# Expert numbers loaded twelve at a time on TensorE, row numbers four at a time on SyncE

## The reference

```
weights, indices = _gate(xt, gate_w)          # 4 experts of 16 for each of the 4096 tokens
h1 = jnp.einsum('td,edi->tei', xt, w1)
h3 = jnp.einsum('td,edi->tei', xt, w3)
a = jax.nn.silu(h1) * h3
y = jnp.einsum('tei,eid,te->td', a, w2, c)
z = jax.nn.silu(xt @ ws1) * (xt @ ws3) @ ws2
```

## Time and profile before

| | |
|---|---|
| median of the runs | 646.26 us (640.41 to 646.84) |
| span of the profiled execution | 669.7 us |
| expert stage in it | 272.6 to 551 us |
| PE busy | 512.2 us, 76% of the span |
| DVE busy | 428.0 us, 64% |
| ACT busy | 303.6 us, 45% |
| POOL busy | 289.2 us, 43% |
| DMA in the expert stage | 0.57 to 0.88 of the 16 engines, turn by turn |

### The profile page before, as it was taken

The page is one execution under the profiler, slowest core; times in us unless marked ns, Lnnn a source line. Parts: engine busy times, 40 slices in busy tenths (PEclk is TensorE's granted clock), DMA queues, the critical chain, the costliest instruction groups (busy, mean ns, idle before and its releaser), DMA issues.

```text
span 669.7 us, 13463 instructions
## 1 busy us (share of the span) xinstructions
PE 512.2 (76%) x3532; PEld 356.3 (53%) x3555; DVE 428.0 (64%) x1200; ACT 303.6 (45%) x659; POOL 289.2 (43%) x334
## 2 busy tenths in 40 slices
PE   1899897697889768879898878878989799645500
PEld 1355454354554435767787666767868675311300
DVE  2446874657766487767677444567878774653784
ACT  3526554245452434456666555655756563101100
POOL 1000107273753720345455330245656464776573
PEclk9999898697998899999999999999999999877755
DMA  7022256354653220378788887578798864342232
GB/s 200 27 79 80 70 182 236 134 188 159 259 199 140 79 86 1 118 246 261 235 283 286 284 282 245 181 238 265 242 298 256 273 218 138 90 131 81 95 119 101
DMA packets 64091, 118.63 MB, mean 177 GB/s; under 512 B 9760, under 2 KB 23088, under 8 KB 64048
## 3 DMA queue, kind: packets, MB, share of 16 engines
q1 hardware_dynamic: 51216, 84.55, 38.5%
q0 software_dynamic: 12288, 33.57, 15.7%
q10 hardware_dynamic: 544, 0.00, 0.0%
HBM read 55.17 MB, written 62.91 MB: 176 GB/s over the span
## 4 chain that ended last, share of the span: by engine, by line
PE 37%; DVE 17%; issue 13%; SPq 10%; DMA 7%; another core or an unknown queue 6%; ACT 5%; POOL 4%; ACTq 0%; DVEq 0%; POOLq 0%
PE t L1346 5%; PE h_even L1155 4%; PE h_even L1157 3%; PE h_even L1156 3%; PE y L1192 3%; DMA kv<-expert_in 3%; PE h_odd L1157 3%; PE h_odd L1155 3%; SPq L327 3%; PE h_odd L1156 3%; DVE x_all L1061 2%; SPq L330 2%; SPq L334 2%; ACT x_all L516 1%
## 5 line engine op out<-in xcount | busy, mean ns | idle before, releaser
L440 POOL DMA_INDIRECT expert_in<-x_all,slots x128 | 129.5, 1012 | 119.8 <-PE h_even L1157 59.5
L459 POOL DMA_INDIRECT wa_stage<-expert_out,result_of x64 | 64.2, 1004 | 39.0 <-issue 14.0
L1346 PE MATMUL t<-ident,kv 128*128 128x128 f32 x384 | 58.5, 275 | 16.2 <-DMA kv<-expert_in 11.7
L1050 DVE TENSOR_TENSOR wa_lo<-bias_heads,wa_hi 128x256 bf16<-128x256 f32 x96 | 40.6, 423 | 46.2 <-ACT wa_hi L648 35.5
L426 POOL TENSOR_SCALAR neg_mean<-mv 128x4 f32<-128x4 f32 x16 | 4.9, 309 | 132.7 <-DVE mv L705 132.5
L459 POOL DMA_INDIRECT q_fm<-expert_out,result_of x32 | 32.2, 1007 | 57.9 <-PE h_odd L1157 34.0
L1031 DVE TENSOR_TENSOR xsT_lo<-t,xsT_hi 128x512 bf16<-128x512 f32 x72 | 49.4, 687 | 11.2 <-ACT xsT_hi L623 6.2
L1346 PEld LDWEIGHTS t<-ident,kv 128*128 128x128 f32 x384 | 43.6, 141 | 23.5 <-issue 11.9
L1155 PE MATMUL h_even<-xsT_hi,we_hi 128*128 128x256 f16 x192 | 52.3, 273 | 0.1
L1156 PE MATMUL h_even<-xsT_lo,we_hi 128*128 128x256 bf16 x192 | 52.3, 273 | 0.0
L1157 PE MATMUL h_even<-xsT_hi,we_lo 128*128 128x256 f16 x192 | 52.3, 273 | 0.0
(11 more groups left out here) (222 smaller groups left out, 1498.9 us busy)
## 6 DMA issues: line engine op xcount, KB each, us to landing
kv<-expert_in SPq DMA_DIRECT2D x96, 256.0 KB
expert_out<-k_exp SPq DMA_DIRECT2D x48, 256.0 KB
expert_out<-q_exp SPq DMA_DIRECT2D x48, 256.0 KB
expert_in<-wa_stage SPq DMA_DIRECT2D x16, 512.0 KB
expert_in<-wa_stage SPq DMA_DIRECT2D x32, 256.0 KB
stage<-in_L_ffn_w SPq DMA_DIRECT2D x48, 128.0 KB
x_in<-in_L_attn_x SPq DMA_DIRECT2D x8, 512.0 KB
out<-gated SPq DMA_DIRECT2D x8, 512.0 KB
```

Source lines behind the costliest of these rows:

```text
L440: pool.indirect_dma_start(xs_dram[b // WB], bass.IndirectOffsetOnAxis(ap=slots[:, b, t, j:j + 1], axis=0), x_all[:, b, t, :], None).then_i ...
L459: pool.indirect_dma_start(y_got[i][:, j, :], None, ys_dram[w], bass.IndirectOffsetOnAxis(ap=result_of[:, b, t, j:j + 1], axis=0)).then_inc ...
L1050: dve.tensor_tensor(aT_lo[r % 2][:, :], a_pair, aT_hi[r % 2][:, :], ALU.subtract).then_inc(at_lo_ready, 1)
L1346: last = pe.transpose(t_bank[r % 2][:, c * 2 * P + i * P:c * 2 * P + (i + 1) * P], xs[r][:, i, c * P:(c + 1) * P], ident[:, :])
```

## The change

On TensorE `chunk_of` goes and `chunks_of(first, n)` comes: one load instruction that fills n registers from n words that lie side by side. A turn calls it once, at its start, for 12 pairs: the two last of the turn before, its own eight, and two more that it does not use. Turn 0 loads 8. On SyncE `ring_rows(w, q)` loads the four row numbers of a group ahead of the group's first `load_xs`. The call checks every value that it loads, as the single load did.

```
-            def load_xs(w, p, r, first=False):
-
-                row = sp.value_load(pair_row[0:1, NPAIR * w + p, :], min_val=0, max_val=SLOTS - PAIR)
+            def ring_rows(w, q):
+
+                return nc.values_load_multi_w_load_instructions(
+                    pair_row[0:1, bass.ds(NPAIR * w + RING * q, RING), 0], engines=[mybir.EngineType.SP],
+                    min_val=0, max_val=SLOTS - PAIR)[1]
+
+            def load_xs(w, p, r, row, first=False):
+
                 if not first:
                     sp.wait_ge(xs_transposed, NPAIR * w + p - RING + 1)
...
+                rows = ring_rows(w, q + 1)
                 for r in range(RING):
-                    load_xs(w, RING * (q + 1) + r, r)
+                    load_xs(w, RING * (q + 1) + r, r, rows[r])
...
-            def chunk_of(g):
-                return pe.value_load(pair_chunk[0:1, g, :], min_val=SHARED, max_val=NCH - 1)
+            def chunks_of(first, n):
+
+                return list(nc.values_load_multi_w_load_instructions(
+                    pair_chunk[0:1, bass.ds(first, n), 0], engines=[mybir.EngineType.PE],
+                    min_val=SHARED, max_val=NCH - 1)[1])
...
-                chunks = [chunk_of(RING * q)]
+                if late(q, 1):
+                    chunks = chunks_of(RING * q - RING, 3 * RING)[RING - 2:]
+                else:
+                    chunks = [None, None] + chunks_of(0, 2 * RING)
                 for i in range(2 * RING):
...
-                    up_pair(g, r, chunks[i])
-                    if i < 2 * RING - 1:
-                        chunks.append(chunk_of(g + 1))
-                    if i >= 2:
-                        down_pair(g - 2, (r - 2) % RING, chunks[i - 2])
-                    elif late(q, 1):
-                        down_pair(g - 2, (r - 2) % RING, chunk_of(g - 2))
+                    up_pair(g, r, chunks[i + 2])
+                    if i >= 2 or late(q, 1):
+                        down_pair(g - 2, (r - 2) % RING, chunks[i])
                 return chunks[-2:]
```

More of the change, by code:

```diff
@@ L357, in _ @@
             sp.wait_ge(kv_summed, NB)
+            rows = ring_rows(0, 0)
             for r in range(RING):
-                load_xs(0, r, r, first=True)
+                load_xs(0, r, r, rows[r], first=True)
             group(0, 0, first=True)
@@ L371, in _ @@
             sp.wait_ge(zero_filled[1], FILLED)
+            rows = ring_rows(1, 0)
             for r in range(RING):
-                load_xs(1, r, r)
+                load_xs(1, r, r, rows[r])
                 store_ys(0, RING * last + r - 3, (r + 1) % RING)
+            rows = ring_rows(1, 1)
             for r in range(RING):
-                load_xs(1, RING + r, r)
+                load_xs(1, RING + r, r, rows[r])
                 if r < RING - 1:
```

## The result

The changed kernel is slower: 678.32 us, the median of 4 runs (676.81 to 680.16), beside 646.19 us for the kernel before in the same session, a ratio of 1.050 with a 95% interval of 1.046 to 1.054. The prediction was 693 us in a range of 649 to 708, with "slower" at 0.76. A ratio here is formed from a kernel's runs in the faster of its two states alone, while a median is of all its runs, so the two need not agree to the last digit.

The account below looks back on a forecast made before the run. PE was taken to bound the expert stage, lacking in good part its sequencer's register work. Longer start gaps and lost clock, less gaps removed, summed to +48.6 us on 669.7, scaled to +47, or 693 us; range 649 to 708.

Parts of the forecast that it names:

- rival (c): Turn starts: checks in a row run at 0.15 us each, start gap 2.3 us, no clock lost: 638 us; chance 0.10.
- I take word by word, 2.6 us: TensorE's load of twelve reads each word separately, so eleven more words add 2.6 us at a turn's start; chance 0.52.
- The price of a piece, 0.24 us: Register loads: the read of each word was taken as 0.24 us, from SyncE's single load of 0.27 us.
- 6.3: PE's idle gap at each turn's start in us: 0.65 + 3.1 for checks + 2.6 for the load.
- the sum: Changes over all turns of the expert stage added up: +48.6 us on the profiled 669.7 us, 7.3%.
- SyncE's 51.8: Turns 4 and 5: SyncE would need 55.4 - 3.6 = 51.8 us after its grouped loads, PE 55.2.
- No longer slower than the others: Expected sign in the profile: turns 4 and 5, 55.4 us together before, would stop being slower than the other turns.
- Rival (b): Turn starts: load of twelve costs as one, 3.7 us gap leaves the clock full: +3, 649 us; chance 0.16.
- 12 x 1.7 = 20: Clock term: behind each turn's start gap PE runs at half clock for 3.3 us, losing 1.7 us a turn.
- 0.9 us a group: SyncE: grouping a group's four loads takes 2.4 instead of 3.3 us, saving 0.9 us, 1.8 a turn.
- rival (a): Turn starts: load of twelve costs as one, gap 3.7 us, clock falls: +18.4, 664 us; chance 0.22.
- the forecast's own range: Whole kernel: 680 to 708 us, for 0.20 to 0.27 us a word and the clock low once or twice a turn.

Follow-up runs that it names:

- Experiment 4: Changed kernel with the load of twelve kept, but each check moved to where its value is next used, ten checks a turn: 638.55 us, ratio 0.982 to the kernel before.
- experiment 6: Changed kernel with the load of twelve kept and TensorE's checks of its values left out: 632.96 us, ratio 0.981 to the kernel before.
- the second profile of before: The kernel before, unedited, profiled once more: 645.21 us, span 643.5 us, against a span of 669.7 us in its first profile.
- the earlier trace: The trace of the kernel before that the prediction read, span 669.7 us; PE's clock fell behind a 4.1 us gap there.
- experiment 3: Changed kernel with TensorE's loads put back to one for each pair, SyncE's grouped loads kept: 645.63 us, ratio 0.999 to the kernel before.
- experiment 5: Changed kernel with two loads a turn, six values at its start and four ahead of its fifth pair, all checked at once: 665.06 us, ratio 1.032 to before.
- experiment 9: Changed kernel with 26 further checked loads of 1 to 12 values ahead of turn 0; only load lengths were asked for, such as 0.86 us for an aligned twelve.
- experiment 11: Changed kernel with three aligned loads of four a turn, each check where its value is next used: 669.56 us beside 666.25 for the kernel before, ratio 1.004.
- 12: Changed kernel with three aligned loads of four a turn and no checks on TensorE or SyncE: 654.9 us beside 666.25 for the kernel before, ratio 0.977.
- experiment 7: Changed kernel with a load of three values at a turn's start, then single checked loads behind each `up_pair`: 647.08 us, ratio 0.999 to the kernel before.
- experiment 8: Changed kernel with the load of twelve and its checks done twice at the start of each loop turn and the last: 733.52 us in a single run.
- experiment 10: Changed kernel with unread matmuls of 512 columns between a turn's twelve checks: 690.55 us beside 666.25 for the kernel before, ratio 1.033.

## Why the prediction came out as it did

**Where and in which form: right.** The loss is all in the expert stage, in one gap at each turn's start in front of the transposes, put down to issue. The gaps ahead of `down_pair` are gone, the waits for rows are fewer. The checks are 0.28 us apart also in a row, which leaves rival (c) without its condition. Experiment 4 shows by moving the checks, and 6 by leaving them out, that they carry the loss.

**The load of twelve: mis-sized.** The step that failed is "I take word by word, 2.6 us". The price of a piece, 0.24 us, was right; that four values can be one piece was not seen. The eleven further values cost 0.86 - 0.31 = 0.55 us. The start gap became 3.8 us on average in turns 1 to 11 instead of 6.3: 2.05 of the difference is this term. The other half microsecond is probably that a start had hardly any gap before on average (the second profile of before has 1.0 us in all, not 0.65 each as in turn 7).

**The near hit is in part luck.** With 0.55 in the sum, nine turns lose 2.05 us less each, 18.5; turn 0, whose load of eight took 0.79 us, 1.2 less; and in turns 4 and 5 PE would need 51.1, so that SyncE's 51.8 would bind: another 3.4 less. The sum is then 48.6 - 18.5 - 1.2 - 3.4 = 25.5, or 671 us on the median. So the load was some 22 us too much, and the rest of the sum some 7 us too little; the forecast is 15 off because the two have opposite signs.

**By turns**, after against the second profile of before:
- Turns 2, 3, 7, 8, 9: 125.8 against 108.3 us, +17.5 (predicted +28.3). A turn is 25.2 instead of 27.6, less by the 2.5 us of the gap.
- Turns 1, 6, 10: 79.3 against 70.6, +8.7 (predicted +10.9, or 4.8 with the right load). Turn 10 still waits 4.1 us for rows, which the sum let pass in the start gap.
- Turns 4, 5: 55.1 against 53.7, +1.5 (predicted -0.2, with 55.2 for PE). The long start is nearly free there: 8.8 us of start gaps came, while the waits for rows fell from 6.5 to 1.4 us and the gaps ahead of `down_pair` went. SyncE's queue now waits for others for 7.8 us in these two turns instead of 2.5, so it is no longer the late one. But the number came out by the load's 4.1 us too much: the clock was low for 6.8 us in each of the two turns, not 3.3, and some waits for rows stayed. "No longer slower than the others" was wrong, too: at 28.2 and 27.0 us they are the second and the fourth longest.
- Turn 0: 22.5 against 19.4, +3.1 (predicted +2.8).
- Turn 11, up to its last transposes: +1.9 (predicted +6.8 for the whole turn). Its start gap was 3.4 us and the clock stayed full.

**The clock: right in total, not turn by turn.** It fell in ten of the twelve turns, though seven of the ten gaps were no longer than the 4.1 us of the earlier trace rows. The exceptions are turns 1 and 11, with gaps of 3.0 and 3.4 us, where turn 10's 3.0 us was enough. Rival (b) took the 4.1 us for a bound, and that does not hold. It stayed low for 6.8 us in six turns and 3.4 in four, not 3.3 throughout. By the count of the low stretches it cost some 20 us more than before, where the sum had 12 x 1.7 = 20.

**SyncE: the saving was next to nothing.** 0.9 us a group was counted. Its load of four took 0.31 us, less than supposed, and still experiment 3 shows 1.3 us at most in turns 4 and 5 and no change in the median. That is where rival (a) fails: it had the start right (3.7 us predicted, 3.8 measured) but came to 664, 14 us short. Half of that is turns 4 and 5, which it let gain 5.4 us where they lost 1.5; most of the rest is turns 1, 6 and 10, +3.1 in it and +8.7 measured.

The measured 678 lies midway between rival (a)'s 664 and the forecast of 693, just under the 680 at which the forecast's own range began: the gap of (a), with more loss around it than (a) allowed.

**Left open:** what stretches the load (0.85 to 2.0 us in the changed kernel, up to 4.0 in experiment 5). It was never stretched with idle DMA engines (experiment 9), but a busy share alone does not do it, as turn 8 shows; in the changed kernel only turns 1 to 4 have it (0.91 to 2.0 us). Open too is how the loss divides between clock and gap beyond the estimate, and why experiment 11 waits more for rows than experiment 4.

## What to carry to other kernels

One instruction for many loads does not make the work one instruction: count what is issued for each value (here a check of 0.28 us) and ask where it lands. Spread behind matmuls one at a time it was mostly hidden; gathered at a turn's start, where the sequencer has no lead, all of it stood in the open, and PE's clock was lost behind the gap as well. Keep the gathered load, leave each check where its value is first used or drop it where the range is proven, and start multi-value loads at a multiple of 16 bytes: that was 1.8 to 2.3% faster than the kernel before in experiments 4, 6 and 12 (with their intervals, 0.9 to 3.5%). It is no guarantee: experiment 11 follows the same advice with three loads a turn and gained nothing.

## What was new about the hardware

- A register load of several values from SBUF takes about 0.06 us plus 0.23 to 0.28 for each piece, and a piece is four values if the load starts at a multiple of 16 bytes, one value if it starts elsewhere or the value is left over behind the fours: 0.86 us for an aligned twelve, 1.47 for an unaligned six.
- The same load of twelve took up to 2.0 us in the changed kernel and 3.0 in experiment 6, and an unaligned six up to 4.0, all within the expert stage. Beside idle DMA engines (share 0.03) no load was stretched, but an aligned twelve took 0.86 us at a share of 0.89, too.
- PE's granted clock fell from 2.4 to 1.2 GHz behind gaps of 1.7 to 2.4 us in some turns of experiment 7, not behind one of 3.4 us in the changed kernel, and stayed there for some 3, 7 or 10 us, 10 only behind gaps of 7.8 to 9.4 us of experiment 8.
- With matmuls between the checks it stayed up at ten of the eleven filled starts of experiment 10, over 3.7 us of checks; the eleventh followed a wait of 1.5 us for VectorE.
- Two executions of one kernel entered the expert stage 10 us apart. A sum on a single profile inherits that.
